# Order of the two products inside each slot of an attention loop

## The reference, cut to what matters

```python
# x: (16, 256, 512), mask: (16, 512) of zeros and ones, Wq, Wo: (256, 256)
NH, dk = 8, 32
q = xt @ Wq.T                                     # xt: (16, 512, 256)
qh = q.reshape(B, T, NH, dk).transpose(0, 2, 1, 3)
scores = scale * einsum('bhqd,bhkd->bhqk', qh, qh)
logits = (scores * cmask + (1.0 - cmask) * NEG) * rmask
ctx = einsum('bhqk,bhkd->bhqd', softmax(logits), qh)
out = transpose(ctx @ Wo.T)                       # (16, 256, 512)
# then a feed-forward part on out: a router takes the best 2 of 8 experts per
# token, the experts and a shared expert are summed, and x is added
```

## Time and profile before

| what | value |
|---|---|
| median of 3 runs | 1340.28 us |
| the profiled execution | 1340.52 us |
| its span, first to last instruction | 1338.6 us |
| TensorE busy | 1228.1 us (92% of the span) |
| VectorE, ScalarE, GpSimd busy | 684.0, 530.6, 694.7 us |
| mean granted TensorE clock | 0.947 of full speed |
| logit products (L536) | 512, mean 557 ns |
| key products (L548) | 512, mean 406 ns |
| reduces (L710) | 512, mean 684 ns |
| exponentials (L649) | 512, mean 596 ns |

### The profile page before, as it was taken

One profiled execution on the slowest core, in us unless ns is written; L12 is line 12 of the kernel. 1 busy time (PEld: TensorE's weight loads), 2 busy tenths in 40 slices (PEclk: granted clock), 3 DMA queues, 4 the chain that ended last, 5 costly groups with the idle time before them and its releaser, 6 DMA issues. The chain is left out here.

```text
span 1338.6 us, 21991 instructions
## 1 busy us (share of the span) xinstructions
PE 1228.1 (92%) x5564; PEld 687.0 (51%) x5565; DVE 684.0 (51%) x1178; ACT 530.6 (40%) x992; POOL 694.7 (52%) x602
## 2 busy tenths in 40 slices
PE   5899999999999999999814799999999999899998
PEld 2445544545455444544314344444444444489997
DVE  4676676667767666777179112221222122136666
ACT  1465566656656665656410222222222222221211
POOL 1487787778778777878638222222222222034543
PEclk7799999999999999999855799999999999989999
DMA  6645644554555456442081332233222222158886
GB/s 177 180 132 151 160 134 125 153 159 126 143 159 144 118 157 159 123 116 73 16 327 66 98 99 84 89 94 94 85 88 94 93 88 85 71 171 271 282 275 226
DMA packets 93921, 183.54 MB, mean 137 GB/s; under 512 B 11664, under 2 KB 14224, under 8 KB 93888
## 3 DMA queue, kind: packets, MB, share of 16 engines
q1 hardware_dynamic: 81856, 145.38, 36.3%
q0 software_dynamic: 10880, 35.66, 8.5%
q10 hardware_dynamic: 1152, 2.10, 0.6%
HBM read 129.02 MB, written 51.97 MB: 135 GB/s over the span
## 5 line engine op out<-in xcount | busy, mean ns | idle before, releaser
L710 DVE TENSOR_REDUCE row_max<-bank 128x1 f32<-128x512 f32 x512 | 343.5, 684 | 179.8 <-PE bank L536 179.1
L649 ACT ACTIVATE probsT<-bank 128x512 f32<-128x512 f32 x512 | 300.1, 596 | 233.2 <-PE bank L548 231.0
L408 POOL TENSOR_TENSOR key_sum<-key_sum,probsT 128x1024 f32<-128x1024 f32 x128 | 299.5, 2368 | 0.4 <-ACT probsT L649 0.4
L536 PE MATMUL bank<-k_stack,q_stack 96*128 96x512 f32 x512 | 283.3, 557 | 13.2 <-DMA q_stack<-q_hi 6.4
L1238 PE MATMUL bank<-gate_up_sb,rows_T 128*128 x576 | 273.1, 597 | 1.6 <-ACT rows_T L1173 1.6
L404 POOL TENSOR_TENSOR key_sum<-probsT 128x1024 f32<-128x1024 f32 x64 | 151.3, 2377 | 131.3 <-ACT probsT L649 131.3
L548 PE MATMUL bank<-q_stack,k_stack 99*128 99x512 f32 x512 | 207.2, 406 | 1.3 <-ACT probsT L649 1.1
L536 PEld LDWEIGHTS bank<-k_stack,q_stack 96*128 96x128 f32 x512 | 98.9, 194 | 170.7 <-DVE row_max L710 126.2
L1238 PEld LDWEIGHTS bank<-gate_up_sb,rows_T 128*128 128x128 f32 x576 | 104.6, 192 | 106.4 <-issue 106.4
L1124 POOL COPY row_prob<-slot_prob 128x1 f32 (+1 forms) x72 | 13.1, 182 | 258.4 <-DVE rows_scaled L1139 255.3
L558 PE MATMUL bank<-probsT,vals 128*32 128x512 f32 x1024 | 136.5, 605 | 0.1
(11 more groups left out here) (141 smaller groups left out, 1531.6 us busy)
## 6 DMA issues: line engine op xcount, KB each, us to landing
expert_rows_dram<-rows_out SPq DMA_DIRECT2D x72, 256.0 KB, 2.1
k_stack<-hi_dram SPq DMA_DIRECT2D x60, 256.0 KB, 4.1
q_stack<-hi_dram SPq DMA_DIRECT2D x60, 256.0 KB, 6.5
x_row<-in_x SPq DMA_DIRECT2D x16, 512.0 KB, 3.6
hidden_dram<-hid SPq DMA_DIRECT2D x16, 512.0 KB, 4.9
gate_up_sb<-in_L_ffn_gate_up_w SPq DMA_DIRECT2D x8, 1024.0 KB, 12.6
tok<-hidden_dram SPq DMA_DIRECT2D x16, 512.0 KB
x_in<-in_x SPq DMA_DIRECT2D x16, 512.0 KB
```

The source lines that it names most:

```text
L408: nc.gpsimd.tensor_tensor(total, total, probs(k), ALU.add).then_inc(added, 1)
L536: nc.tensor.matmul(logit_bank[i % 2][:, :], q_stack[par][g][0:K_LOGIT, h, q * P:(q + 1) * P], k_stack[par][g][0:K_LOGIT, h, :], start=True ...
L649: nc.scalar.activation(probsT[:, j, :], key_bank[j % 2][:, :], ACT.Exp, scale=SCALE).then_inc(probs_ready, 1)
L710: nc.vector.tensor_reduce(row_max[g][:, i:i + 1], logit_bank[i % 2][:, :], AX.X, ALU.max)\
```

## The change

Inside the slot loop of the program of TensorE the call of find_keys moves ahead of the call of find_logits. All other engines' programs stay, and so do the semaphores and their counts.

```diff
                 for s in range(2 * NJ):
                     g, j = divmod(s, NJ)
                     du, i = divmod(j + LEAD, NJ)
+                    find_keys(b, par, g, j)
                     if exists(kind, g, du + 1):
                         find_logits(*place(b, par, g, du + 1), i)
-                    find_keys(b, par, g, j)
                     use_misc(b, kind, par, s)
```

## The result

The swapped kernel takes 1351.59 us (median of 4 runs, 1347.08 to 1352.66) against 1339.01 us of the kernel before. The ratio is 1.0086, with a 95% interval from 1.0058 to 1.0114: it is slower, by 0.6 to 1.1%, where 0.24% had been forecast. The profiled execution is the fastest of the four, 1347.08 us with a span of 1345.2.

A forecast was written before the change was run, and what follows sets the result against it. TensorE's instruction stream was taken to bound the loop (busy 523.20 of 540 us), so only its waits counted. Terms 3.3 + 0 + 0 - 0.1 = +3.2 us on 1340.28 gave 1343.5 us, range 1339.3 to 1347.4.

The forecast's parts named there:

- Step 1, the mechanism: Router product in slot 28, 14 rows: chain from slot 26's logit product starts 0.24 us later; +3.3 us in all.
- the turn's delay: Turn of the maxima in slot 27 comes 0.24 us later, but under the router product's wait, adding nothing.
- Step 2, slot 13: Logit product held by slot 11's reduce, 15 rows: later reduce offset by the key product going ahead; 0 us.
- The rival that had a chance of 0.15: Slot 13's held logit product ends the pair later, at full 0.24 us per row: 1346.9 us; chance 0.15.
- Step 3, the projection: Projection in slot 20, 14 rows, waits for ScalarE's copy into vals, which gets no earlier: 0 us.
- Step 4, row 0: The ends: key product fills 0.24 us of slot 11's DMA wait, slot 0 may lose 0.1 to 0.2; together -0.1 us.
- The 2.2 us of margin for the stores of the maxima: SP's stores of max_hi and max_lo come 0.24 us later, still 2.2 us before next row's slot 0 needs them: 0.
- The clock: Rival: longer router wait drops TensorE to 1.2 GHz to each row's end, 14 x 5 = +70 us, about 1411; chance 0.01.

The follow-up runs named there:

- one reciprocal more: Kernel before, old order, with one extra independent VectorE reciprocal behind the transposed reciprocal of slot 26, in rows with a router product: 1341.3 us, ratio 1.0011.
- swap, again: The swapped kernel unchanged, run once more: 1348.2 us, ratio 1.0056 to the kernel before.
- three reciprocals more: Kernel before, old order, with three extra VectorE reciprocals behind the transposed reciprocal of slot 26: 1353.8 us, ratio 1.0114.
- the swap with the chain moved: Swapped kernel with VectorE's reciprocal and its transpose for slot 25's sums moved behind max_lo in slot 27: 1336.7 us, ratio 0.9987.
- the three that are filled: Swapped kernel, router product's first part in slot 29: 1335.6 us; old and new order with that, reciprocal behind max_lo, values' turn in slot 18: 1324.0 and 1323.9 us.

## Why the prediction was wrong

**Step 1, the mechanism:** right. The swap lengthens the router's chain, in 14 rows. The size of the standstill was right too: 0.21 to 0.22 us per row for 0.24, so 2.9 us for 3.3 (14 x 0.24 is 3.36, which the prediction writes as 3.3). Its place was half right. I had said that the turn's delay lies under the router's wait and costs nothing of its own, and that the router's wait grows from 0.73 to 0.97. It grew to 0.83, and the other 0.12 stands before the turn. The sum is the same because the router's end is set by VectorE either way.

**Step 2, slot 13:** right at 0, by the pair's end and by the kernel with the swap everywhere but in slot 26. The rival that had a chance of 0.15 for it did not come.

**Step 3, the projection:** right at 0. Its waits are 5.2 us before and after.

**Step 4, row 0:** not settled. Its standstill for the DMA differs from run to run by more than the 0.1 us that was forecast. The 2.2 us of margin for the stores of the maxima held in row 7, but not in row 0: there the key product of slot 0 of the next row waits 0.29 us for them in the swapped kernel (at 81.72), and none did before.

**The clock is the step that failed.** I had the case among the rivals, at a chance of 0.01 and a price of 70 us, and both were wrong. The reason given was that "in the loop the granted clock was 1.00 throughout, with 0.73 us of standstill per row". That showed what happens at 0.73 us, not how far it is from there to a fall. The runs have it: no fall at 0.73; none at 0.83 in one place (one reciprocal more, a single profile); one or two per profile with 0.83 and another 0.12 before the turn (the swap); four with 1.04. And it was priced as if it came in every row and lasted to the row's end. It comes in few rows, and a long one costs 4.7 to 4.8 us:

| kernel | from the router product ahead of the fall to the next, us | without a fall | more |
|---|---|---|---|
| swap | 43.87 | 39.14 | 4.7 |
| swap, again, row 1 | 43.89 | 39.15 | 4.7 |
| swap in slot 26 alone | 43.89 | 39.13 | 4.8 |
| three reciprocals more, rows 4, 9 and 10 | 43.97, 43.91, 43.91 | 39.22 | 4.7 |
| three reciprocals more, the short one, row 8 | 40.79 | 39.22 | 1.6 |

With the 9.4 to 12.6 us that the swap costs against the kernel before, 2.9 for the chain leaves 6.5 to 9.7, that is 1.4 to 2.1 falls of 4.7 us in a mean execution. The two profiles of the swap have one and two. So the term that was missing is 4.7 us times 1.4 to 2.1; the number of falls is read off the result and could not have been worked out from the kernel before.

Nine falls were seen in the four profiles that had any. Eight of them, the seven long ones among them, began 0.9 to 2.2 us after the start of a router product that had waited (1.2 in the profile after, 1.4 and 1.2 in its repeat); the ninth, in row 0, began 0.4 us after the logit product that had waited there for the same chain. Why it is one row and not another stays open.

The Trainium skill (TensorE: Matmul & The Clock Gate, HAM oscillation) describes gaps that recur and drop TensorE's clock. Its gaps are waits for DMA several times as long as the ones here, so it does not say that this change was at risk, as the prediction read it; the runs agree with it only in kind. What the page describes is a fall at every gap, and here it comes, with the swap, at one gap in seven to fourteen. That the clock depends on the standstill and not on the order is shown by the kernel with three reciprocals; that a filled or shorter standstill keeps the clock up agrees with four kernels in which no fall came (the swap with the chain moved, and the three that are filled), of which three have the new order. How far the old kernel is from the edge was not measured finer: no fall at 0.73 and in the one profile at 0.83 us of standstill per row, falls at 0.95. Only one execution of each run has a profile. The two of the kernel before that have one, 1340.5 and 1341.7 us, are among its slower ones and have no fall; in the others none can be ruled out.

## What to carry to other kernels

Swapping two instructions of equal length on a full TensorE is worth only what it does to the chains that end in a TensorE wait: list those waits, follow each back to the pair, and the other slots can be forgotten. A standstill that recurs and has not cost the clock so far is no proof of safety a tenth of a microsecond further on; price the clock as some falls of several us each, and not as never or always. The gain lay in the same list: putting ready work where TensorE waits brought 1.1%, and in the kernels so filled the order of the pair made no difference.

## What the runs showed of the hardware

A standstill of TensorE of about 1 us in a row of 39 us, with the engine otherwise full but for 0.4 us before the projection, is enough for the granted clock to fall from 2.4 to 1.2 GHz now and then: four times in 14 rows at 1.04 us, once or twice with the swap (0.83 and 0.12), never at 0.73 us in the two profiles of the kernel before. Seven of nine falls lasted 10.2 us, although TensorE was busy all through them; the two others lasted 3.4.

An instruction of VectorE that no one waits for and that depends on nothing took 0.21 us by its record (128 x 16 elements), but the next started 0.13 us behind it, and the router's wait grew by 0.10; three of them took 0.36 us from the first's start to the next instruction's. As a brake of a known size it had to be measured first.
